# Preactivated convolution and rotation on one core: band loads and stores of the first sum on ScalarE's queue, one engine for the first normalisation, averages before statistics, partial loads before the second sum

## The reference

```python
x = x + conv5x5_depthwise(gn(x), weight)          # x: [16, 128, 64, 64], NCHW
x = x + einsum('hvc,bchw->bvhw', R, gn(x))        # R: [64, 128, 128], one matrix per image row h
# gn: per image and per group of 4 channels, (v - mean) / sqrt(var + 1e-5) over 4*64*64 values
```

## Time and profile before

| what | us |
|---|---|
| median of 3 runs (lowest, highest) | 558.55 (557.21, 558.85) |
| the profiled execution: its own time | 558.65 |
| its span, from the first to the last instruction | 556.8 |
| TensorE busy | 450.6 |
| ScalarE busy | 361.4 |
| VectorE busy | 347.2 |
| GpSimd busy | 186.0 |
| time of the packets of the DMA queue used, share of 16 engines' span | 92.0% |

### The profile page before, as it was taken

The page is one execution under the profiler, slowest core; times in us unless marked ns, Lnnn a source line. Parts: engine busy times, 40 slices in busy tenths (PEclk is TensorE's granted clock), DMA queues, the critical chain, the costliest instruction groups (busy, mean ns, idle before and its releaser), DMA issues.

```text
span 556.8 us, 8400 instructions
## 1 busy us (share of the span) xinstructions
PE 450.6 (81%) x3024; PEld 172.8 (31%) x3024; DVE 347.2 (62%) x649; ACT 361.4 (65%) x598; POOL 186.0 (33%) x299
## 2 busy tenths in 40 slices
PE   0169999999898898989899899962998778788772
PEld 0123333333333333333333233321443333333330
DVE  3426787877876876686778768561574544544533
ACT  1066887787777678768877888842675455455550
POOL 0223534433533533353344335301343233233230
PEclk9999999999999999899899999995899998998997
DMA  6898788989889888889988989937999999999999
GB/s 155 200 201 167 204 218 222 244 220 226 244 216 226 225 225 216 219 216 235 223 224 243 226 224 308 274 85 235 375 394 397 394 396 397 396 398 396 395 394 325
DMA packets 214329, 150.03 MB, mean 269 GB/s; under 512 B 138384, under 2 KB 179472, under 8 KB 214288
## 3 DMA queue, kind: packets, MB, share of 16 engines
q1 hardware_dynamic: 214288, 149.49, 92.0%
HBM read 82.14 MB, written 67.33 MB: 268 GB/s over the span
## 4 chain that ended last, share of the span: by engine, by line
SPq 30%; DMA 28%; DVE 13%; ACT 12%; PE 11%; issue 4%; DVEq 0%
SPq L165 23%; DMA out_dram<-area 21%; ACT area L305 8%; PE ps L434 7%; DMA area<-tap_lines 7%; DVE stats L382 3%; DVE area L365 3%; DVE area L414 3%; DVE stats L389 3%; SPq L179 2%; PE ps L482 2%; ACT area L294 2%; SPq L227 2%; ACT area L322 2%; SPq L172 1%
## 5 line engine op out<-in xcount | busy, mean ns | idle before, releaser
L434 PE MATMUL ps<-area 64*64 64x512 f32 x2560 | 297.8, 607 | 8.5 <-ACT area L322 8.5
L267 POOL TENSOR_SCALAR area<-area,affine 128x256 f32<-128x256 f32 x192 | 132.9, 707 | 222.1 <-DVE affine L375 222.1
L305 ACT ACTIVATE area<-ps 64x512 f32<-64x512 f32 x256 | 150.4, 587 | 10.6 <-PE ps L434 5.9
L482 PE MATMUL ps<-area 128*128 128x512 f32 x256 | 123.7, 630 | 34.9 <-ACT area L343 28.1
L434 PEld LDWEIGHTS ps<-area 64*64 64x64 f32 x2560 | 93.2, 134 | 158.5 <-issue 156.9
L414 DVE TENSOR_TENSOR area<-ps,area 128x512 f32<-128x512 f32 x128 | 81.2, 685 | 85.7 <-DMA out_dram<-area 68.6
L335 ACT ACTIVATE area<-area,norm 128x256 f32<-128x256 f32 x160 | 82.1, 588 | 72.2 <-DMA area<-x_scratch 58.5
L365 DVE TENSOR_TENSOR area<-area 128x1024 f32<-128x1024 f32 x64 | 78.8, 1232 | 77.1 <-ACT area L305 77.0
L294 ACT ACTIVATE area<-area 64x1280 f32<-64x1280 f32 x64 | 81.3, 1270 | 60.1 <-DMA area<-tap_lines 59.2
L279 POOL TENSOR_SCALAR area<-area,norm 128x256 f32<-128x256 f32 x96 | 52.0, 555 | 132.9 <-DMA area<-x_scratch 81.0
L389 DVE BATCH_NORM_STATS2 stats<-area 128x6 f32<-128x512 f32 x128 | 79.9, 685 | 10.8 <-DMA area<-in_x_dram 10.8
(11 more groups left out here) (22 smaller groups left out, 38.3 us busy)
## 6 DMA issues: line engine op xcount, KB each, us to landing
area<-in_x_dram SPq DMA_DIRECT2D x256, 128.0 KB, 3.3
x_scratch<-area SPq DMA_DIRECT2D x64, 512.0 KB, 6.0
area<-x_scratch SPq DMA_DIRECT2D x32, 1024.0 KB, 12.4
out_dram<-area SPq DMA_DIRECT2D x32, 1024.0 KB, 11.3
area<-tap_lines SPq DMA_DIRECT2D x32, 330.0 KB, 5.1
tap_lines<-line SPq DMA_DIRECT2D x1, 200.0 KB, 3.1
norm_scratch<-affine SPq DMA_DIRECT2D x8, 2.0 KB
rot_all<-_L_conv_rota_matrix_dram SPq DMA_DIRECT2D x4, 0.5 KB, 10.4
```

Of the source, the lines that this page charges most:

```text
L267: last = nc.gpsimd.tensor_scalar(padded[k % GRING][:, :, j, PAD:PAD + W], xin[k % XRING][:, j], affine[:, k, 0, 0, j:j + 1], affine[:, k, ...
L305: last = nc.scalar.activation(y[k % YRING][rows, 2 * pair + c], ps[half, bank + n].rearrange("p (j w) -> p j w", j=J), ACT.Identity)
L434: last = nc.tensor.matmul(ps[half, bank + n], taps[k % 2][rows, 2 * pair + c, d], padded[k % GRING][rows, 2 * pair + c, :, d:d + W], start ...
L482: nc.tensor.matmul(ps[:, m % 6, :], rot_t[u % 2][:, h], gn[n % NRING][:, h], start=True, stop=True).then_inc(rotated, 1)
```

## The change

1. The store of the tap lines, the taps loads and the stores of the first sum are issued by ScalarE. In step s it does: root of round s+1; two stores of group s-2; the taps load of group s+1 (for s of 1 and more; groups 0 and 1 before the steps); evict; turn taps of group s+1; evict. SP keeps the input loads, `store_norms` and the rotations.
2. GpSimd normalises all 8 image pairs of the first stage; ScalarE none.
3. On VectorE the deviations of round s+2 come before the input statistics of group s+3.
4. The granule ring has 7 buffers. Granules 0 to 4 are loaded in two parts: channels 0 to 111 ("early": after the stores of groups 0 to 27 and after the `xin` buffer that the granule covers is free), channels 112 to 127 ("late": after all stores). Both parts stand in SP's program behind its loop over s. The norms are loaded after them.

```diff
@@ SP
-            for k in range(2):
-                load(k)
-            sp.wait_ge(line_ready, len(POS_IDX + NEG_IDX))
-            sp.dma_start(tap_lines, line[:]).then_inc(line_stored, 16)
-            load(2)
-            load(3)
-            sp.wait_ge(line_stored, 16)
-            load_taps(0)
-            load_taps(1)
-            for k in range(4, XRING - 1):
+            for k in range(XRING - 1):
                 load(k)
@@
-                if group(s + 2):
-                    sp.wait_ge(taps_ready, 2 * (s + 1))
-                    load_taps(s + 2)
-                if group(s - 1):
-                    sp.wait_ge(x1_ready, 2 * s)
-                    store(s - 1)
                 if group(s - 3) and (s - 2) % NBATCH == 0:
                     store_norms(s - 2 - NBATCH)
@@
+            early, late = slice(0, EARLY_GROUPS * GC), slice(EARLY_GROUPS * GC, C)
+            for k in range(YRING):
+                sp.wait_ge(x1_stored[k], 32 * (EARLY_GROUPS // YRING))
+            for n in range(EARLY):
+                sp.wait_ge(x1_ready, 2 * (XRING * ((GROUPS - 1 - EARLY_SLOTS[n]) // XRING) + EARLY_SLOTS[n] + 1))
+                load_granule(n, early).then_inc(in_landed[n], 16)
+            for k in range(YRING):
+                sp.wait_ge(x1_stored[k], 32 * (GROUPS // YRING))
@@
-            load_granule(0)
+            for n in range(EARLY):
+                load_granule(n, late).then_inc(in_landed[n], 16)
             sp.wait_ge(norm2_stored, 32 * (GROUPS // NBATCH))
             sp.dma_start(norm2[:], norm2_dram).then_inc(norm2_landed, 16)
-            for n in range(1, IRING):
-                load_granule(n)
+            for n in range(EARLY, IRING):
+                load_granule(n, slice(0, C)).then_inc(in_landed[n], 16)
@@ GpSimd
-                    for j in range(POOL_J):
+                    for j in range(J):
@@ ScalarE
+            act.wait_ge(line_ready, len(POS_IDX + NEG_IDX))
+            act.dma_start(tap_lines, line[:]).then_inc(line_stored, 16)
+            act.wait_ge(line_stored, 16)
+            load_taps(0)
+            load_taps(1)
@@
+                if group(s - 2):
+                    act.wait_ge(x1_ready, 2 * (s - 1))
+                    store(s - 2)
+                if group(s + 1) and s >= 1:
+                    act.wait_ge(taps_ready, 2 * s)
+                    load_taps(s + 1)
                 if group(s - 1):
                     evict(s - 1, 1)
                 if group(s + 1):
                     k = s + 1
                     turn_taps(k)
-                    act.wait_ge(affine_ready, k + 1)
-                    for j in range(POOL_J, J):
-                        last = nc.scalar.activation(padded[k % GRING][:, :, j, PAD:PAD + W], xin[k % XRING][:, j],
-                                                    ACT.Identity, scale=affine[:, k, 0, 0, j:j + 1],
-                                                    bias=affine[:, k, 0, 1, j:j + 1])
-                    last.then_inc(normed_act, 1)
                 if group(s):
                     evict(s, 0)
@@ VectorE, step s: the block below moves from ahead of "if is_round(s + 2)" to behind it
+                if group(s + 3):
+                    k = s + 3
+                    dve.wait_ge(x_landed[k % XRING], 16 * 2 * GC * (k // XRING + 1))
+                    for q in range(J // 2):
+                        last = nc.vector.bn_stats(
...
+                if is_round(s + 3):
+                    last.then_inc(stats_ready, 1)
```

More of the change, by code:

```diff
@@ L33 @@
 ROUNDS = GROUPS + 4
-POOL_J = 6
 NBATCH = 8
@@ L41 @@
 GCOLS = RH * J * W
-IRING = 6
+IRING = 7
+EARLY = 5
+EARLY_SLOTS = (4, 5, 6, 0, 1, 2, 3)
+EARLY_GROUPS = 28
 ORING = 4
@@ L80, in conv_rotate_kernel @@
         used[0] = 0
-        tin = [piece((RH, J, W)) for _ in range(IRING)]
+        slots = [piece((RH, J, W)) for _ in range(IRING)]
+        tin = [slots[n] for n in EARLY_SLOTS]
         tout = [piece((J, RH, W)) for _ in range(ORING)]
@@ L124, in conv_rotate_kernel @@
         normed_pool = sem("normed_pool")
-        normed_act = sem("normed_act")
         convolved = sem("convolved")
@@ L150, in group, with granule_landings @@
             return 0 <= g < GROUPS
+        def granule_landings(n):
+            return 16 * (n // IRING + 1) + (16 if n % IRING < EARLY else 0)
         def is_round(r):
@@ L167, in load @@
                                      ).then_inc(x_landed[slot], 16)
[L169 to L180, removed]
             def store_norms(first):
@@ L218, in _, with load_granule @@
                     sp.dma_start(rot_all[:, rows], rota_src[:, rows]).then_inc(rot_landed, 16)
-            for n in range(YRING):
-                sp.wait_ge(x1_stored[n], 32 * (GROUPS // YRING))
-            def load_granule(n):
+            def load_granule(n, channels):
                 u, half = n // 2, n % 2
[L225 to L229, removed]
+                return sp.dma_start(tin[n % IRING][channels].rearrange("p h j w -> p h (j w)"),
+                                    x1_dram[channels, u * RH:(u + 1) * RH, half * J:(half + 1) * J, :].rearrange(
+                                        "c h j w -> c h (j w)"))
+            early, late = slice(0, EARLY_GROUPS * GC), slice(EARLY_GROUPS * GC, C)
[6 more added lines that the diff above has]
+                sp.wait_ge(x1_stored[k], 32 * (GROUPS // YRING))
             def store_granule(n):
@@ L244, in _ @@
                 if n + IRING < GRANULES:
-                    load_granule(n + IRING)
+                    load_granule(n + IRING, slice(0, C)).then_inc(in_landed[(n + IRING) % IRING], 16)
             for n in range(ORING):
@@ L274, in _ @@
             for n in range(GRANULES):
-                pool.wait_ge(in_landed[n % IRING], 16 * (n // IRING + 1))
+                pool.wait_ge(in_landed[n % IRING], granule_landings(n))
                 if n >= NRING:
@@ L287, in _, with load_taps, store @@
             nc.scalar.activation(warm[:], eps[:], ACT.Sqrt)
+            def load_taps(k):
+                window = bass.AP(tensor=tap_lines.tensor, offset=k * GC * LINE,
+                                 ap=[[1, H], [LINE, GC], [1, WINDOW]])
+                act.dma_start(taps_raw[k % 2][0:H].rearrange("p c d h -> p c (d h)"), window
+                             ).then_inc(taps_landed[k % 2], 16)
+            def store(k):
+                for n in range(2):
+                    rows = slice(n * HALF, (n + 1) * HALF)
+                    dst = x1_dram[k * GC:(k + 1) * GC, :, n * J:(n + 1) * J, :].rearrange("c h j w -> h c (j w)")
+                    act.dma_start(dst, y[k % YRING][rows].rearrange("p c j w -> p c (j w)")
+                                 ).then_inc(x1_stored[k % YRING], 16)
+            act.wait_ge(line_ready, len(POS_IDX + NEG_IDX))
[3 more added lines that the diff above has]
+            load_taps(1)
             def turn_taps(k):
@@ L330, in _ @@
             for n in range(GRANULES):
-                act.wait_ge(in_landed[n % IRING], 16 * (n // IRING + 1))
+                act.wait_ge(in_landed[n % IRING], granule_landings(n))
                 if n >= NRING:
@@ L384, in _ @@
                             in_=y[(s - 1) % YRING][:, :, 2 * q:2 * q + 2].rearrange("p c j w -> p c w j"))
[L385 to L393, removed]
                 if is_round(s + 2):
@@ L405, in _ @@
                                                    ).then_inc(spread_ready, 1)
+                if group(s + 3):
[3 more added lines that the diff above has]
+                        last = nc.vector.bn_stats(
+                            out=stats[:, k % 2, 0, 2 * q:2 * q + 2].rearrange("p j f -> p (j f)"),
+                            in_=xin[k % XRING][:, 2 * q:2 * q + 2].rearrange("p j c w -> p (c w) j"))
+                if is_round(s + 3):
+                    last.then_inc(stats_ready, 1)
                 if group(s):
@@ L427, in convolve @@
                     pe.wait_ge(normed_pool, k + 1)
-                    pe.wait_ge(normed_act, k + 1)
                 if 2 * k + pair >= PAIRS:
```

## The result

The changed kernel takes 609.7 us (607.7 to 610.7, 4 runs) against 558.7 of the kernel before: a ratio of 1.090 (95% interval 1.085 to 1.096), slower by 51 us. The forecast was 613 in a range of 572 to 645. The profiled execution has a span of 607.1 us, 50.3 more than before.

A forecast was written before the change was run, and what follows sets the result against it. SP's DMA queue was taken to set the 10.57 us step. Last matmul at 415.1 + 2 for rotation loads + (556.8 - 369.7) + 7.5 for the second stage gave a 611.7 us span, so 613 us, range 572 to 645.

The forecast's parts named there:

- What bounds the kernel before: First stage: SP's queue sets the 10.57 us step; at most about 1 us a step can be won.
- Part 1, the loop of the taps: ScalarE's step: taps load issued behind two stores in the step that turns it, making a step of 12.6 us.
- X: ScalarE's step: time from the first store's issue to the taps' landing, taken as 7.3 us, bounds 5.3 and 8.3.
- The 5.3 behind X: Rest of ScalarE's step: root 0.2, turn and evict of pair 0 5.05, wake-up about 0.05 us.
- ScalarE held in its issues: Rival: two of ScalarE's three DMA issues held 1 us each, step 14.6 us, time 671 us; chance 0.09.
- the prediction's own signs of being wrong: Forecast fails if taps land within 5 us, ScalarE's issues aren't near 0.6 us, or early loads start before matmuls end.
- Part 3, "worth nothing there": VectorE's new order: spread ready 2.5 us sooner, near A+9, ahead of the turn at A+10.1, so no gain.
- Part 2: GpSimd's eight images take 5.7 us and end near A+6.7, before the turn ends, so it costs nothing.
- The start: First group starts at 19.5 us, 13 us earlier, counting no second group's statistics between averages, root and scale.
- Part 4: Second stage: early loads stand behind SP's loop, so aren't early, and delay the norms; sum +7.5 us.
- The term of 10.6 us: Second stage: 4.2 MB more ahead of the norms at 397 GB/s makes them 10.6 us later.
- The rival "faster": Taps do not queue behind the stores: step 10.6, time 555.5 us, 0.5% faster; chance 0.11.

The follow-up runs named there:

- the two edits that leave SP's queue as it is: Kernel before with only VectorE's order changed: 556.6 us; kernel before with only GpSimd normalising all 8 image pairs: 556.5 us.
- one swap: Changed kernel with the taps load issued ahead of the two stores on ScalarE: 555.3 us, ratio 0.997 to the kernel before.
- both repairs: Changed kernel with taps load ahead of the stores, and granules loaded whole with norms behind granule 0: 536.8 us, ratio 0.960; with VectorE's old order 604.4 us.
- whole granules: Changed kernel with the second stage's old order: granule 0 whole, norms, granules 1 to 6 whole, ring of 7: 592.6 us, ratio 1.063.

## Why the prediction was right, and where its steps were not

- **What bounds the kernel before.** Borne out, though not by one edit alone: the two edits that leave SP's queue as it is gave 2 to 2.5 us, and with the taps load off that queue and ahead of the stores the step was 9.9 to 10.0 us. Those kernels also have parts 2 and 3, and without part 3 the step is 12.0.
- **Part 1, the loop of the taps.** That the place behind the stores makes the loop was right, and shown by one swap (609.7 to 555.3). Both terms were off, with opposite signs. X is 8.4 us in the step shown and 9.1 in the mean, not 7.3, and above the upper bound of 8.3. The prediction let the taps wait for the stores' data; by the medians X is 1.3 us of store issues, 2.0 of the taps' own issue and 5.3 from there to the landing. The 5.3 behind X is 2.6 to 2.8, since ScalarE issues its DMAs while the evicts of pair 0 run. So 1.8 too little and 2.5 too much left the step at 11.9 (11.74 on TensorE) beside a forecast of 12.6: that it is near is luck.
- **ScalarE held in its issues**, given 0.09 as a rival, is true in part: the taps' issue costs 2.0 us and not 0.6, one of the prediction's own signs of being wrong. In the changed kernel the wait for taps covers what it costs ScalarE, but it delays the landing by 1.4 us a step. Where the taps load comes a step early, ScalarE's standing still is part of what sets the step, at 3.04 us.
- **Part 3, "worth nothing there".** Wrong, and the largest error of mechanism: 39 us here, 68 with both repairs. I checked VectorE's spread against the time the taps need, and overlooked that the root which waits for the spread stands ahead of the DMA issues in ScalarE's program. Nor did TensorE's wait for the spread go away: it is 1.10 us before the variance at 221.77.
- **Part 2.** Nothing, as forecast, to within 2.5 us on the kernel before; it wasn't undone in the changed one.
- **The start.** 26.2 instead of 19.5. The step "now without the second group's statistics between" was wrong: they still stand ahead of round 0's scale, and they came later than before. VectorE's timeline:

```profile
18.80 2.50 DVE L402 BATCH_NORM_STATS2 stats<-area 128x6 f32<-128x512 f32 x4 [5.23 <-DMA area<-in_x_dram]
21.22 0.18 DVE L374 RECIPROCAL affine<-std 128x8 f32<-128x8 f32 x1
```

  The spread of round 0 is done at 13.6, its reciprocal follows at 21.2, behind the statistics of group 1, whose input landed 4.1 us later than the 14.71 in the timeline of before. In between, the tap lines and two taps loads ran on the other queue; that these cost the 4.1 us is argued, not shown.
- **Part 4.** The order was read rightly: early loads that aren't early, norms behind them. Its price, 7.5 us, was 20.4, of which 16 are the partial loads and their place (shown by whole granules). The term of 10.6 us, 4.2 MB at 397 GB/s, failed: partial loads run at 281 and at 105 to 107.
- **The rival "faster"** did not occur; its condition, X below 5.4, was far off.

## What to carry to other kernels

Before a DMA moves to another queue, write down what stands ahead of it there and how long before its use it is issued: a short load that is needed at once belongs ahead of long stores. On an engine that computes and issues DMAs, an issue may go out beside activations that still run, but not before a wait in front of it has ended, and an order on another engine that ends this wait can be worth more than its own time. A load called early is as early as the last wait in its queue, and cutting a DMA by partitions has a price in bandwidth that must be paid out of idle time.

## What the runs showed of the hardware

- DMAs with runs of 2 KB moved at 385 to 397 GB/s over 128 partitions, 281 over 112, 209 over 64 and 105 to 111 over 16, with the DMA share at 1.05 to 1.11 in each (0.96 for the quiet pair of stores). The DMAs' size falls with the partitions, from 1 MB to 128 KB.
- The issue of a taps load on ScalarE takes 0.60 us ahead of two stores and 2.0 behind them (medians). From the end of the issue to the landing it is 5.1 and 5.3 us, and 5.5 with no stores in ScalarE's queue.
- ScalarE issues a DMA beside activations that stand ahead of it in its program and still run: the store at 211.29 beside an evict that ends at 213.7. A wait ahead of the DMA holds it (208.15 instead of about 206).
